# Loops over batches written out, a narrower bias spread, and the softmax guard as Exp's bias column

## What is computed

```python
qkv = x @ W_attn.T + b_attn                    # x: 4 batches x 1024 tokens x 256
q, k, v = split(qkv)                           # 16 heads of 16
att = einsum('bhqd,bhkd->bhqk', q, k) * (1.0 / sqrt(D))
att = att + rel_emb[buckets(relative position)]    # per head
att = where(causal, att, -inf)
y = einsum('bhqk,bhkd->bhqd', softmax(att), v)
x = layernorm(x + y @ W_proj.T + b_proj)
x = layernorm(x + ffn(x))                      # two routed experts and a shared one
```

## Time and profile before

| | us |
|---|---|
| median of 3 runs (lowest, highest) | 987.3 (985.47, 989.46) |
| the profiled execution | 986.67 |
| its span, first to last instruction | 984.9 |
| PE busy in the span | 840.3 (85%) |
| DVE busy | 556.4 (56%) |
| ACT busy | 568.3 (58%) |
| POOL busy | 252.7 (26%) |
| mean granted PE clock | 0.935 |

### The profile page before, as it was taken

The page is one execution under the profiler, slowest core; times in us unless marked ns, Lnnn a source line. Parts: engine busy times, 40 slices in busy tenths (PEclk is TensorE's granted clock), DMA queues, the critical chain, the costliest instruction groups (busy, mean ns, idle before and its releaser), DMA issues. The chain is left out here.

```text
span 984.9 us, 18061 instructions
## 1 busy us (share of the span) xinstructions
PE 840.3 (85%) x6689; PEld 600.2 (61%) x6689; DVE 556.4 (56%) x1160; ACT 568.3 (58%) x733; POOL 252.7 (26%) x200
## 2 busy tenths in 40 slices
PE   7269926999998799999678899889996999999993
PEld 5157712343333333333367888779886999998993
DVE  3348864665765465566587756674552355445543
ACT  4247725888888688888634453453342445454451
POOL 4224431000100100020145452444142233333333
PEclk9679966999999799999989999999998999999997
DMA  7785557566856565593291111111036444443301
GB/s 154 91 295 189 177 128 134 114 112 107 125 97 111 93 114 96 100 136 54 52 248 55 55 55 55 44 50 60 22 142 227 158 163 151 151 151 132 127 23 43
DMA packets 61806, 112.96 MB, mean 115 GB/s; under 512 B 9412, under 2 KB 50409, under 8 KB 56297
## 3 DMA queue, kind: packets, MB, share of 16 engines
q1 hardware_dynamic: 56824, 99.07, 43.2%
q0 software_dynamic: 4896, 12.73, 3.5%
HBM read 58.15 MB, written 30.82 MB: 90 GB/s over the span
## 5 line engine op out<-in xcount | busy, mean ns | idle before, releaser
L873 ACT ACTIVATE probs<-slots 128x1024 f32<-128x1024 f32 x288 | 275.0, 1031 | 49.2 <-DVE slots L942 39.9
L942 DVE TENSOR_TENSOR slots<-slots,bias_t 128x512 f32<-128x512 f32 (+1 forms) x288 | 159.2, 604 | 77.8 <-PE slots L975 75.9
L1644 DVE TENSOR_TENSOR h_lo<-h_f,h_hi 128x512 fp32r<-128x512 f32 x136 | 104.6, 771 | 129.7 <-PE o_ps L1742 78.8
L993 PE MATMUL o_ps<-probs,v_st 128*32 128x256 f32 (+1 forms) x2560 | 155.5, 365 | 0.8 <-ACT probs L873 0.8
L993 PEld LDWEIGHTS o_ps<-probs,v_st 128*32 128x32 f32 x2560 | 67.5, 110 | 77.8 <-issue 48.8
L975 PE MATMUL slots<-q_first,k_st 99*128 99x512 bf16 (+3 forms) x384 | 83.5, 343 | 31.6 <-DVE v_st L887 16.0
L1484 ACT ACTIVATE h_f<-slots,b_cur 128x512 f32<-128x512 f32 x72 | 49.5, 688 | 102.6 <-PE slots L1728 91.6
L1484 ACT ACTIVATE h_f<-slots,b_c 128x512 f32<-128x512 f32 x64 | 44.0, 687 | 95.6 <-PE slots L1728 94.0
L1488 ACT ACTIVATE h_hi<-h_f 128x512 fp32r<-128x512 f32 x136 | 86.0, 632 | 4.3
L975 PE MATMUL slots<-q_second,k_st 99*128 99x512 bf16 (+3 forms) x384 | 80.5, 329 | 7.7 <-ACT probs L873 7.7
L1045 POOL TENSOR_TENSOR y_t<-y_t,rs_row 128x2048 f32 (+1 forms) x4 | 18.2, 4562 | 258.5 <-DMA rs_row<-rsum_d 258.5
(11 more groups left out here) (207 smaller groups left out, 1889.8 us busy)
## 6 DMA issues: line engine op xcount, KB each, us to landing
qk_d<-parts SPq DMA_DIRECT2D x32, 384.0 KB, 2.6
cur_hi<-experts_hi SPq DMA_DIRECT2D x9, 1024.0 KB, 4.8
cur_lo<-experts_lo SPq DMA_DIRECT2D x9, 1024.0 KB, 7.2
k_st<-qk_d SPq DMA_DIRECT2D x16, 384.0 KB
q_first<-qk_d SPq DMA_DIRECT2D x48, 128.0 KB
q_second<-qk_d SPq DMA_DIRECT2D x48, 128.0 KB
xs_sb<-xs_d SPq DMA_DIRECT2D x9, 528.0 KB, 5.1
bs_sb<-base_d SPq DMA_DIRECT2D x9, 512.0 KB, 4.0
```

Of the source, the lines that this page charges most:

```text
L873: nc.scalar.activation(probs[:, k % PBUFS, :, 0:w], slots[:, k % SLOTS, :, 0:w], ACT.Exp).then_inc(exped, 1)
L942: ins = dve.tensor_tensor(tile, tile, bias_t[:, h0:h0 + 2, first:first + w], ALU.add)
L993: ins = pe.matmul(o_ps[32 * j2:32 * j2 + 2 * D, half, q:q + w], v_st[:, g, j, j2, :], probs[:, (k + j2 // 2) % PBUFS, j2 % 2, col:col + w] ...
L1644: dve.tensor_tensor(h_lo[:, n % 3], h_f[:, q % 2], h_hi[:, n % 3].bitcast(F32), ALU.subtract).then_inc(hl_ok, 1)
```

## The change

Six things, in the attention half.

- Every loop over batches is written out: `batches` calls the body four times in place of `rolled`.
- by_dist is spread to 16 copies, not 128. The spread is issued in tile 0 after the x_in load, and bias_t is filled by eight reads of 16 partitions each, two behind the stores of each of tiles 1 to 4.
- guard_d is zeroed from a tile of zeros with 1536 columns, not by broadcasting 128. The guard rows then stay zero unless `wide` is set.
- POOL's masking of bias_t stands before the last batch of tiles.
- SP loads the q and k parts and the guard rows of unit 0 before the last batch's stores. The guard's fill and its write to guard_d are gone.
- The guard is spread to neg_guard, a column of 128, zero where `wide` is set, and is the bias operand of Exp. In `attend` PE waits for the ones before the first output only, and DVE copies v for unit 0 first and for the three others behind pair 1 of step 1.

```diff
+ST_DMAS = 10
+SKEW = 16
...
+def load_guard(sp, guard_d, b, g, q_st, loaded):
+
+    rows = guard_d[bass.ds(b, 1)].rearrange("o g h t -> (o g) h t")
+    sp.dma_start(q_st[STACK:KROWS], rows[:, UH * g:UH * g + UH]).then_inc(loaded, 16)
...
-def rolled(eng, last, body):
-
-    body(0, False, True)
-    with eng.Fori(1, last) as i:
-        body(i, True, True)
-    body(last, True, False)
...
+def batches(eng, last, body):
+
+    for b in range(last + 1):
+        body(b, b > 0, b < last)
...
+        zeros = sb("zeros", [P, B * GUARD * H * T // P], BF16)
...
+        bias_rows = nc.dram_tensor("bias_rows", [SKEW, H, 3 * P], F32, kind="Internal").ap()
...
-                flat = guard_d.rearrange("b g h t -> (b g h t)").rearrange("(p n c) -> p n c", p=P, c=P)
-                sp.dma_start(flat, zeros[:, :].unsqueeze(1).to_broadcast([P, B * GUARD * H * T // P // P, P])
+                sp.dma_start(guard_d.rearrange("b g h t -> (b g h t)").rearrange("(p n) -> p n", p=P), zeros[:, :]
                              ).then_inc(guard_out, 16)
 
-                sp.wait_ge(dist_sb, 1)
-                sp.dma_start(bias_rows.rearrange("p h x -> h p x"),
-                             by_dist[:, :].unsqueeze(1).to_broadcast([H, P, 3 * P])).then_inc(dist_out, 16)
-                sp.wait_ge(dist_out, 16)
-                skew = bass.AP(bias_rows.tensor, P, [[3 * P * H - 1, P], [3 * P, H], [1, WIN]])
-                sp.dma_start(bias_t[:, :, :], skew).then_inc(bias_in, 16)
+                def spread_bias():
+
+                    sp.wait_ge(dist_sb, 1)
+                    sp.dma_start(bias_rows.rearrange("p h x -> h p x"),
+                                 by_dist[:, :].unsqueeze(1).to_broadcast([H, SKEW, 3 * P])).then_inc(dist_out, 16)
+
+                def skew_bias(pieces):
+
+                    sp.wait_ge(dist_out, 16)
+                    for a in pieces:
+                        skew = bass.AP(bias_rows.tensor, P - SKEW * a, [[3 * P * H - 1, SKEW], [3 * P, H], [1, WIN]])
+                        sp.dma_start(bias_t[SKEW * a:SKEW * a + SKEW], skew).then_inc(bias_in, 16)
 
                 def body(b, before, after):
                     for t in range(TPB):
@@ -334,20 +345,24 @@
                             nxt = at_tile(x_tiles, n + TPB)
                             sp.wait_ge(xt_ps, n + 1)
                             sp.dma_start(x_in[:, t], nxt).then_inc(x_ld[t], 16)
+                        if not before and t == 0:
+                            spread_bias()
                         for c in range(NC):
                             dst = qk_d[bass.ds(b, 1), c, :, :, TT * t:TT * t + TT].rearrange("o n p t -> p (o n) t")
                             sp.wait_ge(part3, NC * n + c + 1)
                             sp.dma_start(dst, parts[:, t, c]).then_inc(stored[t], 16)
-                rolled(sp, B - 1, body)
+                        if 1 <= n <= P // SKEW // 2:
+                            skew_bias((2 * n - 2, 2 * n - 1))
+                for b in range(B - 1):
+                    body(b, b > 0, True)
+                for t in range(TPB):
+                    sp.wait_ge(stored[t], 16 * NC * (B - 1))
+                load_parts(sp, qk_d, 0, 0, k_st[:, 0], q_first, st_ld[0])
+                sp.wait_ge(guard_out, 16)
+                load_guard(sp, guard_d, 0, 0, q_first, st_ld[0])
+                body(B - 1, True, False)
                 for t in range(TPB):
                     sp.wait_ge(stored[t], 16 * NC * B)
-                load_parts(sp, qk_d, 0, 0, k_st[:, 0], q_first, st_ld[0])
-
-                sp.wait_ge(guard_out, 16)
-                sp.wait_ge(filled, 1)
-                sp.dma_start(guard_d[:, 0].rearrange("b h (a n) -> (h a) b n", a=TPB),
-                             fill[:, :].unsqueeze(1).to_broadcast([H * TPB, B, TT])).then_inc(guard_out, 16)
-                sp.wait_ge(guard_out, 32)
...
-                rolled(pool, B - 1, body)
-                pool.wait_ge(bias_in, 16)
+
+                for b in range(B - 1):
+                    body(b, b > 0, True)
+                pool.wait_ge(bias_in, 16 * P // SKEW)
 
                 pool.affine_select(out=bias_t[:, :, :], in_=bias_t[:, :, :], compare_op=ALU.is_ge, fill=MASKED,
                                    base=0, pattern=[[0, H], [1, WIN]], channel_multiplier=-1).then_inc(bias_ok, 1)
+                body(B - 1, True, False)
...
-                done(dve.tensor_scalar(guard_b[:, :], value(RAW), 0.0, -1.0, ALU.max, ALU.mult))
-                done(dve.tensor_copy(value(GUARD_F), guard_b[:, :]))
-                dve.sem_inc(guard_set, 1)
+                done(dve.tensor_scalar(value(GUARD_F), value(RAW), 0.0, -1.0, ALU.max, ALU.mult))
 
                 done(dve.tensor_scalar(value(LOW1), value(ROOT), SELF_SLACK, value(BIAS), ALU.mult, ALU.add))
                 done(dve.tensor_tensor(value(LOW2), value(LOW1), value(SELF), ALU.subtract))
                 done(dve.tensor_tensor(value(LOW3), value(LOW2), value(GUARD_F), ALU.subtract))
                 done(dve.tensor_scalar(value(FITS), value(LOW3), EXP_BOTTOM, None, ALU.is_le))
+                done(dve.tensor_tensor(value(NEG), value(GUARD_F), value(FITS), ALU.mult))
+                dve.sem_inc(guard_set, 1)
                 done(dve.tensor_scalar(wide[:, :], value(FITS), -1.0, 1.0, ALU.mult, ALU.add))
                 dve.wait_ge(guard_ps, 1)
-                dve.tensor_copy(fill[:, :], o_ps[0:H * TPB, 0, 0:1].to_broadcast([H * TPB, TT])).then_inc(filled, 1)
+                dve.tensor_copy(neg_guard[:, :], o_ps[:, 0, 0:1]).then_inc(filled, 1)
...
-                pe.matmul(o_ps[0:H * TPB, 0, 0:1], one_row[:, 0:H * TPB], tops[:, 7:8], start=True, stop=True
-                          ).then_inc(guard_ps, 1)
+                pe.matmul(o_ps[:, 0, 0:1], one_row[:, :], tops[:, 12:13], start=True, stop=True).then_inc(guard_ps, 1)
...
+                    load_guard(sp, guard_d, 0, 0, q_first, neg_out)
+                    sp.wait_ge(neg_out, 16 * GUARD * (B + 1) + 16)
...
-                    if not (isinstance(b, int) and b + g == 0):
-                        load_parts(sp, qk_d, b, g, k_st[:, buf], q_st[buf], st_ld[buf])
-                    sp.dma_start(q_st[buf][STACK:KROWS], guards[:, UH * g:UH * g + UH]).then_inc(st_ld[buf], 16)
+                    load_parts(sp, qk_d, b, g, k_st[:, buf], q_st[buf], st_ld[buf])
+                    load_guard(sp, guard_d, b, g, q_st[buf], st_ld[buf])
...
-                                                     ACT.Exp).then_inc(exped, 1)
-                rolled(act, B - 1, body)
+                                                     ACT.Exp, bias=neg_guard[:, 0:1]).then_inc(exped, 1)
+                batches(act, B - 1, body)
...
-                for g in range(UNITS):
-                    load_v(0, g)
+                load_v(0, 0)
...
+                        else:
+                            for g_ in range(1, UNITS):
+                                load_v(0, g_)
...
+                        if i == 0 and not before:
+                            pe.wait_ge(ones_ok, 1)
...
-                pe.wait_ge(ones_ok, 1)
```

More of the change, by code:

```diff
@@ L219, with project_in @@
 PRODUCTS = [(0, 0), (0, 1), (1, 0)]
-def rolled(eng, last, body):
-    body(0, False, True)
-    with eng.Fori(1, last) as i:
-        body(i, True, True)
-    body(last, True, False)
-def project_in(nc, slots, o_ps, ident, wp_hi, wp_lo, bp_row, v_all, shared_at, y_at, bias_t, wide, qk_d, guard_d,
+def batches(eng, last, body):
+    for b in range(last + 1):
+        body(b, b > 0, b < last)
+def project_in(nc, slots, o_ps, ident, wp_hi, wp_lo, bp_row, v_all, shared_at, y_at, bias_t, wide, neg_guard, qk_d, guard_d,
                k_st, q_first, st_ld, x_tiles, w_attn, b_attn, w_proj, b_proj, rel_emb, buckets):
@@ L261, in project_in @@
         top = sb("top", [P, 2]); top_bias = sb("top_bias", [H, 1])
-        tops = sb("tops", [1, 16]); guard_b = sb("guard_b", [1, 1], BF16)
+        tops = sb("tops", [1, 16])
         one_row = sb("one_row", [1, P])
-        fill = sb("fill", [H * TPB, TT], BF16)
-        bias_rows = nc.dram_tensor("bias_rows", [P, H, 3 * P], F32, kind="Internal").ap()
+        bias_rows = nc.dram_tensor("bias_rows", [SKEW, H, 3 * P], F32, kind="Internal").ap()
         ld_w = [sem(f"ld_w{n}") for n in range(4)]
@@ L480, in body @@
                                           bv_row[:, :].unsqueeze(1).to_broadcast([P, NB, C]), ALU.add).then_inc(v_ev, 1)
-                rolled(dve, B - 1, body)
+                batches(dve, B - 1, body)
                 take_norms(TILES - 1)
@@ L598, in body @@
                         ins.then_inc(v_ps, 1)
-                rolled(pe, B - 1, body)
+                batches(pe, B - 1, body)
                 norms(TILES - 1)
@@ L606, in _, with exact_maxima @@
                 pe.wait_ge(guard_set, 1)
-                pe.matmul(o_ps[0:H * TPB, 0, 0:1], one_row[:, 0:H * TPB], tops[:, 7:8], start=True, stop=True
-                          ).then_inc(guard_ps, 1)
```

(10 more changed lines are left out.)

15 lines of the change are left out of this document (6 added, 9 removed).

## The result

| | before | after |
|---|---|---|
| median (lowest, highest), 4 runs each | 988.25 (985.47, 989.46) | 947.69 (946.03, 951.17) |
| the profiled execution | 986.67 | 951.17 |
| its span | 984.9 | 949.4 |
| PE busy | 840.3 (85%) | 845.7 (89%) |
| ACT busy | 568.3 | 591.0 |

The changed kernel takes 0.961 of the time before, with a 95% interval of 0.9589 to 0.9632. The forecast was 946.8. The profiled execution is the slowest of the four, so the traces show 35.5 us of gain (984.9 - 949.4) where the medians show 40.6.

A forecast was written before the change was run, and what follows sets the result against it. The prediction took holes without matmuls and, between them, PE and nearly ACT to bound the touched stages. Its terms, -26.8 - 9.4 + 0 - 10.3 + 6 = -40.5 us, gave a forecast of 946.8 us, range 937 to 960.

The forecast's parts named there:

- A: Projections, bias spread: PE's 26.1 us wait for x_in and a 0.65 us slow restart go, -26.8 us.
- B: Handover to attention: guard fill gone, masking moved from the tail to behind tile 5, -9.4 us in sum.
- masking behind tile 5: Projections: POOL's moved masking holds DVE's products and PE's norms, +3.0 us, between 1.0 and 4.5.
- masking out of the tail: End of projections: without POOL's masking beside DVE's squares and selfs, the chain starts 4.5 us earlier.
- the fill: Handover to attention: the guard fill and its 7.6 us landing go, gain 7.9 us.
- C: Start of attention: earlier first adds and later v copies cancel, 0 us, bounds -1.5 and +0.5.
- D: Attention loops written out: without PE's jump back, its standing and slow restart go, -10.3 us.
- E: Exp with a bias column in attention: 90 ns more for each of 288, of which +6 us shows.
- feed-forward: Third stage, not touched by the change and carried over, 0 us.
- the third rival: Projections: masking behind tile 5 costs what the tail gains or waits for skewed reads, 950 to 956 us; chance 0.06.
- The rival that the stall isn't the jump: Attention: the 8.7 us stall isn't PE's jump back and one of that size stays, 957.1 us; chance 0.09.
- The first rival: Attention: ACT becomes the bound and most Exps pay the column's full 0.095 us, 954 to 968 us; chance 0.11.

The follow-up runs named there:

- e6: Changed kernel with the spread at 128 copies again, its new order and eight skewed reads kept: 964.04 us, ratio 0.9768 to before.
- e10: Kernel before with 16 copies and eight skewed reads, all still ahead of the loop's first x_in load: 968.35 us, ratio 0.9848 to before.
- e1: Changed kernel run again, unchanged: 949.44 us, ratio 0.963 to before.
- e3: Changed kernel with POOL's masking of bias_t back behind the last batch of tiles: 944.72 us, ratio 0.9578 to before.
- e5: Changed kernel with mask values set in by_dist before the spread and POOL's masking removed: 943.11 us, ratio 0.9563 to before.
- e8: Changed kernel with the guard handed over by guard rows again, Exp without bias column, part loads kept early: 946.12 us, ratio 0.9585 to before.
- e11: Changed kernel with attention's start as before (PE waits for the ones first, DVE copies all four v units first): 950.68 us, ratio 0.9673 to before.
- e4: Changed kernel with only PE's attention loop over batches a hardware loop again: 957.87 us, ratio 0.9718 to before.
- e7: Kernel before with only PE's attention loop over batches written out: 976.79 us, ratio 0.9905 to before.
- e2: Changed kernel with Exp called without its bias column and the guard not subtracted: 942.23 us, ratio 0.9555 to before.
- e9: Changed kernel with mask values set in by_dist, guard rows again and no Exp bias column: 940.64 us, ratio 0.9564 to before.
- e12: Changed kernel with the projections' loops a hardware loop again on PE, ACT and DVE: 949.19 us, ratio 0.9651 to before.

## Why the prediction was right

Each row is a step of the prediction; the measured value is the difference of the two traces, whose sum is 35.5.

| step | forecast | traces | isolated by |
|---|---|---|---|
| A, x_in wait and slow restart, to the turn of tile 6 | -26.8 | -26.2 | e6, e10 |
| B, masking behind tile 5 | +3.0 | +6.7 | e1, e3, e5 |
| B, masking out of the tail | -4.5 | -3.6 | e3, e5 |
| B, the fill | -7.9 | -7.75 | e8: 2.4 of it in the new order |
| C, start of attention | 0 | -0.2 | e11: -1.5 to -2.0 |
| D and E, loops and column, over attention | -4.3 | -4.1 | e4, e7; e2 |
| feed-forward | 0 | -0.3 | unchanged code |

**A** held. From the turn of tile 1 to that of tile 6 the changed kernel gained 28.0 us: the 26.8, and five tiles whose pitch is 0.25 shorter. Against that, the first load came 0.4 us later and the first tile took 1.4 longer (17.84 against 16.46), because PE's pairs of matmuls took 1.05 us in place of 0.63 until 19.4 us, in before until 16.9. That part isn't the change's: e1 has 16.71. An issue was said to keep SP under 0.5 us, though the earlier trace rows has one of 2.57; the two reads kept it 1.2 to 1.7 a tile, at no cost that shows. The prediction gave the order and the width together one price; e6 and e10 show what either leaves when it is alone: the new order 12.1 us (56.56 against 44.49), the 16 copies 7.8 (52.25 against 44.49). What it didn't see is that the wide spread makes stores late as well: in e6 the cost of 128 copies came through a buffer of parts that ACT wanted back.

**B** contains the term that was mis-sized. The prediction saw that the masking isn't removed but moved, and that DVE's bf16 products are held while it runs; 3.4 us of hold was near the 3.93 less 0.41 measured. But it took the hold for the cost, and even took off something for catching up. Selfs, held next by POOL's subtraction, added 1.0 to the hold. PE ran out of work for 4.33 us, and came back at the low clock: from the norms' first matmul to the first at full clock it took 5.38 us (87.06 to 92.44), the same work a tile later 2.98. The two make 6.7. In step A the same slow restart had been counted; here it was forgotten. Its bound of 4.5 was too low, and the third rival (the masking costs what the tail gains) came true for this part: 6.7 lost, 3.6 gained. The tail's 4.5 was mis-sized as well: it counted the 1.0 us that squares were held, which e5 shows to be a subtraction's and which stays. Two of its numbers don't follow from the terms: 1.0 to 4.5 for the masking gives B from -11.4 to -7.9, not -12.4 to -6, and a masking that costs just the tail's 4.5 gives 948.3, not 950.

**The fill** went as worked out. But the prediction took its 7.6 us for a property of that write. In the three kernels with the part loads behind the stores it lands in 7.6, 7.6 and 7.1 us (before, e7, e10), in both with these loads moved ahead in 1.9 (e8, e9). The likely reading is that the queue in front of it had set the landing, and that moving the loads alone would have won an estimated 5.3 of the 7.75 us (7.75 less the 2.4 that e8 shows). No run moved the loads alone, so this isn't shown.

**D** was measured both ways. The jump cost 10.1 us of pitch before (29.56 against the 19.48 around it) and 10.5 in e4, and taking it out won 9.9 us over attention in e7, by medians 8.4 (e4) and 9.7 (e7), for 10.3 forecast. The rival that the stall isn't the jump has fallen. The Trainium skill's "~51 ns" for Branch-always (Advanced Engine Details and Errata, Control Flow Timing) isn't what PE stands here; the 9.56 us in e4's row is. In e12 the jump of the projections shows no gap. The looped body in attention holds 832 matmuls, that in the projections 124; whether the length decides, no run tests.

**E** was right in both numbers: an Exp of 1123 ns, forecast about 1120, and 6.7 us in all, forecast 6. The first rival, at 13 us or more, fell. The sum agrees, its working only in part: 4.0 us were to show in PE's waits for Exp, and in e2's comparison these differ by 1.4. So the right size is in part luck.

**C** was called nothing, and against before it is. Against its own undo it is a gain of 1.5 to 2.0, beyond the bound of 1.5 at its upper end.

By the traces the forecast was 5.0 us too good: 3.7 of it is the masking, 0.9 the tail, 0.6 step A. By the medians the gain is 40.6 for 40.5 forecast. The two pictures differ because the profiled execution of after is 3.5 above its own median, and that of before 1.6 below; e1's gain, 36.0, is near the traces'. The gain is thus known to some 4 us only, about the size of what B missed. That the forecast lies within 1 us of the median is partly chance; that the time lies in the range of 937 to 960 isn't.

## What to carry to other kernels

Work that is moved still has a price, and in its new place it can be a higher one: where it starves PE, add the stretch at the low clock behind the idle time, not only the idle time. Ask first whether it can go altogether, as the mask did in the 16 rows that were written anyway. Before a slow DMA is designed away, look at what is queued in front of it. Before an operand is added to an instruction that runs 288 times on a nearly full engine, price it against the single step it saves.

## What the runs showed of the hardware

- Beside POOL's masking of 128x4096 (3.90 us in the tail, 4.17 behind tile 5) a bf16 product of 128x512 on DVE took 3.93 us in place of 0.41 and ended 0.3 us after the masking did; beside POOL's subtraction of 128x512 (1.16 us) it took 1.40.
- The same write of 128 KB landed in 1.9 us in e8 and e9, and in 7.1 to 7.6 in before, e7 and e10, which issue nine loads just ahead of it; eight reads of 256 KB landed in a median of 6.0 us when spaced two by two, of 11.0 when issued together.
- PE's jump back stalled it 8.71 and 9.56 us in attention, in a body of 832 matmuls, and not visibly in the projections, in one of 124.
- After 4.33 us without a matmul the granted clock was 0.50 for the next 5.4 us; in e1, after 4.32 us, the slow matmuls ended 4.5 us behind the first.
